# Turned rows copied out of PSUM by ScalarE in front of its counts, in a graph-attention kernel with a sparse adjacency

## The reference

```python
def reference(x, adj, W, attn):            # x (8192, 256) f32, adj (8192, 8192) int32 of 0 and 1
    h = x @ W                              # (8192, 256)
    s1, s2 = h @ attn[:256, 0], h @ attn[256:, 0]
    e = leaky_relu(s1[:, None] + s2[None, :], 0.2)
    e = where(adj > 0, e, -9e15)
    h_prime = softmax(e, axis=1) @ h
    return layernorm(x + elu(h_prime))     # no weights, eps 1e-5
```

## Time and profile before

| | |
|---|---|
| median of 3 runs | 843.47 us (842.3 to 843.72) |
| profiled execution, its own time | 842.7 us |
| its span, first to last instruction | 841.0 us |
| mean granted TensorE clock | 0.872 of full |
| busy: TensorE matmuls, VectorE, ScalarE, GpSimd | 603.0, 631.1, 573.1, 608.5 us |
| DMA | 316 MB, mean 376 GB/s |

### The profile page before, as it was taken

The page is one execution under the profiler, slowest core; times in us unless marked ns, Lnnn a source line. Parts: engine busy times, 40 slices in busy tenths (PEclk is TensorE's granted clock), DMA queues, the critical chain, the costliest instruction groups (busy, mean ns, idle before and its releaser), DMA issues.

```text
span 841.0 us, 10651 instructions
## 1 busy us (share of the span) xinstructions
PE 603.0 (72%) x2585; PEld 389.0 (46%) x2628; DVE 631.1 (75%) x2422; ACT 573.1 (68%) x529; POOL 608.5 (72%) x689
## 2 busy tenths in 40 slices
PE   6589976568776796787867766687658685776761
PEld 4467763235353463554544433445335353553431
DVE  5567653569789888789887598678868776988794
ACT  0055537569869787878787598678869776897710
POOL 4478426778788878777865788888878786887871
PEclk9699999689989998979899798799888897998975
DMA  8999996999999999999999999999999998999711
GB/s 326 403 403 423 423 410 254 417 394 407 414 411 400 396 416 415 415 415 394 408 397 422 401 376 412 404 339 362 416 420 404 414 416 302 404 415 416 289 31 45
DMA packets 61697, 316.00 MB, mean 376 GB/s; under 512 B 19158, under 2 KB 37815, under 8 KB 45248
## 3 DMA queue, kind: packets, MB, share of 16 engines
q1 hardware_dynamic: 36176, 285.49, 83.0%
q0 software_dynamic: 25456, 29.79, 10.7%
HBM read 340.59 MB, written 17.14 MB: 425 GB/s over the span
## 4 chain that ended last, share of the span: by engine, by line
issue 26%; POOL 24%; DMA 22%; DVE 18%; PE 7%; ACT 1%; POOLq 1%; SPq 0%; DVEq 0%; ACTq 0%
POOL GATH L1548 17%; DMA GATH<-haug,ids 5%; DMA WORK<-in_adj_dram,smalls 5%; DMA ADJ<-in_adj_dram 4%; DMA haug<-GATH 4%; POOL GATH L1517 4%; DMA X<-in_x_dram 3%; PE acc L550 3%; PE pk L539 2%; DVE diag L880 2%; DVE smalls L821 1%; DVE PART L890 1%; PE spare L616 1%; DVE Y L925 1%; DVE Y L908 1%
## 5 line engine op out<-in xcount | busy, mean ns | idle before, releaser
L1548 POOL DMA_INDIRECT GATH<-haug,ids x448 | 475.4, 1061 | 131.7 <-issue 128.6
L1368 ACT ACTIVATE WORK<-ADJ 128x4096 bf16<-128x4096 int32 x126 | 454.6, 3609 | 102.5 <-PE pk L539 68.1
L539 PE MATMUL pk<-WORK,D 128*128 128x512 bf16 x981 | 261.8, 416 | 121.4 <-ACT WORK L1368 117.4
L539 PEld LDWEIGHTS pk<-WORK,D 128*128 128x128 bf16 x1024 | 100.4, 104 | 259.7 <-ACT WORK L1368 144.0
L550 PE MATMUL acc<-GATH,diag 128*128 128x256 f32 x512 | 155.3, 458 | 64.7 <-DVE diag L880 64.7
L550 PEld LDWEIGHTS acc<-GATH,diag 128*128 128x128 f32 x512 | 117.0, 234 | 107.7 <-DVE diag L880 83.2
L781 DVE MAX8 smalls<-pk 128x8 f32<-128x512 f32 x64 | 44.5, 695 | 31.9 <-issue 31.9
L890 DVE SCALAR_TENSOR_TENSOR PART<-GATH,smalls,PART 128x256 f32<-128x256 f32 x128 | 62.2, 486 | 4.5
L616 PE MATMUL spare<-X,WORK 128*128 128x256 f32 x256 | 58.9, 384 | 0.0
L1521 POOL DMA_DIRECT2D haug<-GATH x32 | 23.5, 735 | 45.4 <-DVE GATH L772 45.1
L616 PEld LDWEIGHTS spare<-X,WORK 128*128 128x128 f32 x256 | 49.5, 193 | 7.1
(11 more groups left out here) (177 smaller groups left out, 807.1 us busy)
## 6 DMA issues: line engine op xcount, KB each, us to landing
ADJ<-in_adj_dram SPq DMA_DIRECT2D x128, 2048.0 KB, 15.5
haug<-GATH POOLq DMA_DIRECT2D x32, 258.0 KB, 10.5
out_dram<-Y SPq DMA_DIRECT2D x32, 256.0 KB, 9.0
GATH<-haug,ids POOLq DMA_INDIRECT x448
X<-in_x_dram SPq DMA_DIRECT2D x1, 4096.0 KB, 30.7
X<-in_x_dram SPq DMA_DIRECT2D x1, 3072.0 KB, 26.6
X<-in_x_dram SPq DMA_DIRECT2D x1, 1024.0 KB, 6.9
Waug<-in_L_gnn_W_dram SPq DMA_DIRECT2D x1, 256.0 KB, 2.7
```

The lines of the kernel that those rows point to most:

```text
L539: done = nc.tensor.matmul(pk[s % PKS][:], D16[:, k, :], A16[:, q % 2, k * BW:(k + 1) * BW], start=(half == 0 and k == 0), stop=(half == 1 ...
L1368: act.activation(A16[:, q % 2, :], ADJ[:, q % 4, :], ACT.Relu, scale=HALF_SCALE if q % 2 else 1.0, accum_out=degree[:, q // 2, q % 2:q % 2 ...
L1548: pool.indirect_dma_start(out=GATH[:, r, k * DA:(k + 1) * DA], out_offset=None, in_=haug, in_offset=bass.IndirectOffsetOnAxis(ap=ids[:, t ...
```

## The change

copy_xT moves from VectorE to ScalarE. There it is an activation with the function Copy, with the same waits and the same signal. On ScalarE the copies stand in front of the counts: 0 to 5 before count 0, 6 and 7 before count 1, 8 and 9 before count 2, 10 and 11 before count 3, 12 to 14 before count 4, then two each (15 and 16 before count 5, to 23 and 24 before count 9), and 25 to 31 behind count 9, before count 10. In general the copies before count q end with that of group PACK_AFTER[q - 2] + 1. VectorE keeps its order without the copies.

```diff
-            def copy_xT(g):
-                dve.wait_ge(xT_ready, g + 1)
-                if g >= 2:
-                    dve.wait_ge(h_ready, g - 1)
-                dve.tensor_copy(XT[g % 2], xT_ps[g % 2][:]).then_inc(xT_copied, 1)
...
-            copy_xT(0)
-            copy_xT(1)
             pieces = []
             for g in range(G):
                 copy_h(g)
-                if g + 2 < G:
-                    copy_xT(g + 2)
                 if g in (2, 4):
                     mark_first(g // 2 - 1)
...
+            def copy_xT(g):
+                act.wait_ge(xT_ready, g + 1)
+                if g >= 2:
+                    act.wait_ge(h_ready, g - 1)
+                act.activation(XT[g % 2], xT_ps[g % 2][:], ACT.Copy).then_inc(xT_copied, 1)
+
+            def copies_before(q):
+                first = 0 if q < 2 else PACK_AFTER[q - 3] + 2 if q >= 3 else 8
+                last = 8 if q < 2 else PACK_AFTER[q - 2] + 2
+                return range(first if q != 1 else 6, min(last if q else 6, G))
+
             for q in range(2):
+                for g in copies_before(q):
+                    copy_xT(g)
                 act.wait_ge(first_marked, q + 1)
...
             for q in range(2, 2 * EARLY):
+                for g in copies_before(q):
+                    copy_xT(g)
                 count(q)
+            for g in range(PACK_AFTER[2 * EARLY - 3] + 2, G):
+                copy_xT(g)
```

## The result

The changed kernel takes 865.3 us (median of 4 runs, 863.8 to 868.9) against 843.6: a ratio of 1.0262 with a 95% interval of 1.0236 to 1.0289. That is 21.7 us slower; forecast were 863 and a range of 851 to 869.

The account below looks back on a forecast made before the run. TensorE's projection stage was taken to pace the counts and so the adjacency loads, with the ring of stores just under it. 19.5 - 2.0 - 4.9 - 2.6 + 0.9 = +10.9, clock +10.4: 842.7 + 21.3 = 864.0, said 863, range 851 to 869.

Parts of the forecast that it names:

- wait for a copy behind a count: Projection stage: TensorE idles 2.34 us before each of eight projects whose copy stands behind a count on ScalarE.
- price of one, on the distance of the counts: Counts 2 to 9: each waiting project costs 2.44 us, idle plus 0.10 for a slower project; +19.5 us for eight.
- start: First projects and pack(0): copies no longer stand behind VectorE's marks, so project(8) comes earlier; -2.0 us, bounds 0 and -3.5.
- VectorE's waits: Projection stage from 52.51 us: TensorE's waits for VectorE's copies and the stores behind them vanish; -4.9 us.
- clock: TensorE's clock falls to 0.50 behind six or seven of the eight waits, 1.6 us each; +10.4 us, bounds 0 and 13.6.
- hand-over: End of the projection stage: stores land sooner, -2.6 us; counts 10 and 11 and loads 14 and 15 come later, +0.9.
- behind 300 us: After the hand-over: DMA, VectorE and POOL run the same lists, only later, with no change in content; 0.
- faster: Rival: ScalarE's idle time holds the copies, and marks and store waits leave TensorE; 835.8 us, chance 0.04.
- Partly swallowed: Rival: work in the last slices waiting on something else takes up some 5 us; 846 to 851 us, chance 0.08.
- clock kept: Rival: the idle of 2.4 us doesn't bring TensorE's clock down; 853.6 us, chance 0.20.
- worse: Rival: hand-over gains nothing, all eight stalls fall in clock, or low clock outlasts the pack; 870.6 us and up, chance 0.09.
- the unchanged end: Rival: the stage is slower, but the DMA hole is filled by it and the end stays; 842.7 us, chance 0.04.

Follow-up runs that it names:

- one_more_ahead: Changed kernel, with the copies in front of each count reaching one group further, to PACK_AFTER[q-2]+2; 843.7 us.
- filled_waits: Changed kernel, with eight unused identity matmuls in each of TensorE's eight waits for a copy behind a count; 855.3 us.
- hold_half14: Changed kernel, with SyncE asking for half 14 and later ones only when the projection stage's last small stores have landed; 868.2 us.
- late_counts_hold14: Kernel before, with count 10 behind the last copy and half 14 asked for only when the last small stores have landed; 844.2 us.
- counts_among: Changed kernel, with counts 10 and 11 among the last copies, behind copies 26 and 28; 870.1 us.
- both orders mended: Changed kernel, with copies one group further ahead and counts 10 and 11 behind copies 27 and 29; 842.7 us.
- late counts: Kernel before, copies on VectorE, with count 10 (and so 11) waiting until the last copy of turned rows is done; 840.1 us.
- ring of eight: The kernel of both orders mended, with eight buffers for h in place of four; 848.7 us.

## Why the prediction was right

| step | forecast | measured in the profile |
|---|---|---|
| wait for a copy behind a count | 2.34 us, eight times | 2.33 us, eight times (2.76 from the transposes' start, less 0.43); the profile's idle time is 2.16 |
| price of one, on the distance of the counts | 2.44 | 8.52 - 6.09 = 2.43 |
| start | -2.0 | -3.3 (count 2 at 49.49 us) |
| VectorE's waits | -4.9 | gone |
| clock | six or seven falls of 1.6, 10.4 | five falls of 1.68 (10.20 - 8.52), 8.4; 10.0 by the medians with the waits filled |
| end of project(31) | +23.0 | +19.8 |
| hand-over, by the bytes at 300 us | -1.7 | -1.6 (18.2 - 19.8) |
| behind 300 us | 0 | +2.8 (21.0 - 18.2) |
| whole | +21.3 | +21.0 in the span, +21.7 by the medians |

The mechanism was right, and two experiments show its two halves: one_more_ahead takes the wait away and with it the whole loss, filled_waits takes the clock's fall away and leaves the wait. The sum closes: from project(9) at 49.23 us to the end of project(31) are 92.8 us; the content is 64.9, and 8 x 2.44 + 5 x 1.68 = 27.9 is the rest.

Two of the values are less firm than they look. The prediction set its 2.34 us, a distance of starts, beside idle times of the profile, 2.44 and 1.70. On the profile's own scale the new idle time is 2.16, farther from the row that fell than it was put, and the clock indeed fell behind some of the waits only. And the start isn't a fixed gain: in the nine profiled executions of kernels with these copies at the start, count 2 stood between 1.5 and 4.1 us earlier than before.

That the total came within 1 us is partly luck, since two errors cancel. The stage was over-priced by 3.2 us: the start gained 1.3 more, the clock fell less often in this execution. What comes behind 300 us was put at nothing and is 2.8. The hand-over itself came out as a sum, by parts that missed. Its first part went better than said (VectorE took h of group 31 without a wait for a store, count 12 stood 4.7 us less late than project(31) ended, forecast 3.4). The loading left over at count 12 was more than said, 3.1 us by the bytes (18.2 - 15.1) against 1.7. And the prediction left out that the two halves asked for at 142.6 and 146.2 us would be in the way of the last stores, as GpSimd's row shows, so that the first gather came 23.5 us later than before:

```profile
154.52 0.19 POOL L1554 TENSOR_TENSOR smalls<-smalls 128x1 f32<-128x1 f32 x1 [8.53 <-DMA s_row<-WORK]
```

That late gather isn't shown to cost anything: an earlier one gained nothing in hold_half14 nor in late_counts_hold14. By 300 us the kernel is 18.2 us late by its bytes, and counts 40 to 96 start 16.6 to 21.8 us later than before, half of them by 18.8 or more; the last count by 21.1. What makes the last 2 to 3 us isn't settled, nor that they belong to the change: in one_more_ahead counts 40 to 96 stand from 3.9 us earlier to 1.5 later than before, and its last count is 2.4 us later too.

Of the signs that the prediction named, those of the order came: the eight projects, the rows of ScalarE, VectorE waiting for TensorE. Count 12 stood at 146.3 and not near 151 us, by the stage's 3.2 us and the hand-over's 1.3. The clock in the stretches from 60 to 120 us was 0.86, 0.84 and 0.96, in place of 0.75 to 0.85.

One argument of the prediction holds in one direction only. It said that the counts up to 131 us are worth their full time, because the loads follow. Later counts did cost their time, and mostly more: filled_waits, the changed kernel, hold_half14 and counts_among have count 12 late by 5.9, 15.1, 19.5 and 27.2 us and their spans longer by 11, 21, 25 and 27. Only in counts_among, where counts 10 and 11 don't stand behind the last copy, are the two level. Earlier counts gained nothing: count 12 at 119 to 127 us goes with 840 to 849. For the "faster" rival I had put 835.8, and when its condition was made true (one_more_ahead, both orders mended) the time was 843.7 and 842.7. Freed time on TensorE goes into waits for the stores of h, which share the DMA engines with the loads: 26.6 and 31.2 us in those two kernels against 18.4 before. Three runs with unchanged or better counts and a changed share of the engines (late counts -3 us, half 14 held +4 on that, ring of eight +6 on both orders mended) fit the reading that the order of transfers at the hand-over is what is left there, though each of them changes more than that order. "Partly swallowed", "clock kept" and "worse" did not come; nor did the unchanged end.

## What to carry to other kernels

Before work is moved onto an engine with idle time, look at what that idle time waits for and what stands in front of the moved piece in that engine's order: 1.2 us of copies fitted by sum into 2.38 us of idle, and cost 2.4 us a round, because they stood behind a 3.6 us operation that nothing on TensorE needed yet. If a short piece feeds the bottleneck, put it ahead of the long one as soon as its inputs are there; here one group further was enough. And ask separately what a stage's end is worth in each direction: later can cost in full where earlier gains nothing, as it did here.

## What the runs showed of the hardware

The clock of TensorE fell behind waits of 2.16 us, which stood between stretches of full work, and not behind each: five, seven and nine of eight, eight and ten such waits in three executions of the same stage (changed, hold_half14, counts_among). A fall costs 1.7 us of a 10.2 us round, and in the changed kernel the first five rounds had one each and the last three none. Filling 1.95 us of each wait with useless matmuls kept it at 1.00 and was worth 10 us in 865. The Trainium skill (TensorE: Matmul & The Clock Gate, HAM oscillation — how this bites in real kernels) describes a kernel whose clock falls in every single round, behind waits for DMA of about 3 to 5 us. The first five rounds of this trace agree, though its waits are only 2.16 us; the last three don't.

A store of 32 KB (s2) took 1.5 us of GpSimd's wait in the kernel before, with the DMA engines nearly idle (a share of 0.07 at 129 to 131 us), 8.5 us in the changed kernel, where two halves of 2 MB were asked for just ahead of it and just behind it, and 20.8 us in the kernel with the ring of eight, behind loads and stores of h.
